# Masked lanes of a one-hot aggregation get an out-of-range row index, and each indirect gather gets a bound past which rows are skipped

## The chip, the cores and the metric

The kernel runs on one core of one Trainium2 chip. The metric is the device time of one execution in microseconds (us). Before the change it is 5670.04 us, the median of two runs (5664.36 and 5675.72 us).

## The reference

The reference is a stack of four graph layers over 6,250 nodes of 128 features and 106,250 edges, sorted by destination. Each layer takes `h = relu(layernorm(x))`, gathers a row of node data for the source of every edge, and sums something over the edges of each destination:

```python
# layer 0: attention; k, v are per node, q per node
a = (k[src] @ rel_att) . q[dst] * rel_pri / sqrt(16)         # per edge and head
h_agg = segment_sum(v[src] @ rel_msg * softmax_over_dst(a), dst)
# layer 1: degree-normalised sum
h = segment_sum(xs[src], dst)
# layer 2: gated messages
gates = sigmoid(x[src] @ W_src + x[dst] @ W_dst + edge_attr @ W_edge)
out = segment_sum(x[src] @ W_msg * gates, dst) / segment_sum(gates, dst)
# layer 3: mean of neighbours
summed = segment_sum(x[src], dst)
```

What matters here: four times over all edges, a row of a table in HBM is fetched by `src`.

## The kernel before

**Tiles.** Nodes are cut into 49 blocks of 128, plus one spare (`NS` = 50). The edges of a block are cut into tiles of 128 lanes; a tile starts at an edge number that is a multiple of 16, so its first lanes can belong to the block before, and its last lanes to the block after. There is room for `T` = 896 tiles. With this problem's edge list 856 tiles hold edges; the other 40 lie beyond the last edge. Of the 896 x 128 = 114,688 lanes, 106,250 hold an edge of their block and 8,438 (7.4%) do not. 133 tiles have at least one such lane: 40 have nothing else (5,120 lanes), and 93 have 3,318 between them.

**Order.** A pass over the edges takes the tiles in 224 quads of four. They are dealt out so that 16 neighbouring tiles in time lie 8 tiles apart in the edge list, within seven parts of 128 tiles each. The 40 tiles beyond the last edge therefore all fall into the last part, that is in the last seventh of each pass, five of them in every 16.

**The mask.** The prologue fetches, for each tile, 128 source numbers and 128 destination numbers, makes `RELF` (destination minus the block's first node) and `VAL` (1 where `RELF` lies in 0..127, else 0), lines 1118 to 1122. PE transposes `RELF` and `SRCF` so that a tile is a column; DVE copies them to `REL` (fp32) and `SRC` (int32), line 1137. In a pass, DVE makes the one-hot matrix `S` of a quad by comparing `REL` with a row of numbers (line 971). A lane that is not of the block matches nothing, so its row of `S` is zero, and whatever row was gathered for it adds nothing.

**The gathers.** For each quad, SP copies four columns of `SRC` to `ISLOT` (a ring of four slots); POOL waits for it, and for the consumer of the ring slot's last content, and issues four indirect DMAs of 128 rows each, one per tile (line 500):

```python
for j in range(QUAD):
    nc.gpsimd.indirect_dma_start(
        out=rows[:, slot, j, :], out_offset=None, in_=table,
        in_offset=bass.IndirectOffsetOnAxis(ap=ISLOT[:, slot, j:j + 1], axis=0),
    ).then_inc(s["gathered"][slot], 16)
```

There are four passes of 896 gathers: pass 0 (layer 0, table `tab2`, rows of 1,024 bytes), pass 2 (layer 1, `tab1`, 512 bytes), pass 3 (layer 2, `tab2`, 1,024 bytes), and pass 4 (layer 3, `tab1`, 512 bytes). Number 1 belongs to the messages of layer 0, which gather nothing by index. In passes 2 and 4 the ring slot comes free when PE has multiplied it (`agg_done`, line 688); in pass 0 when DVE has multiplied keys by queries (line 1257); in pass 3 when DVE has multiplied messages by gates (line 1331). The results of line 688 are added to an accumulator in SBUF by DVE, one tile at a time (line 988).

**Between the passes.** Layer norms, and projections by PE that write the tables (`dve_proj`, `pe_proj`, `sp_proj`, the latter at line 446). Pass 0 has six seams between its seven parts, at which the running maxima of the softmax are computed (`maxima`, `rescale`). The gathers of pass 0 start when both halves of `tab2` are stored (`proj[0]["stored"]`). `G`, the buffer that receives the gathers, also holds the index windows and the projection's staging in the prologue. POOL clears the accumulators with a memset (lines 537 and 561); DVE waits for that on the semaphore `acc_cleared`.

Of the kernel before, what the change touches and what calls it, by code (L numbers as in the profile page):

```python
# [8 lines left out]
ALU = mybir.AluOpType  # L9
# [3 lines left out]
P = 128  # L13
# [10 lines left out]
GROUP = 16  # L24
NEG = -1e30
PAD_NODE = 1 << 20


class Sizes:
# [25 lines left out]
def wait(eng, sem, value):  # L55

    if isinstance(value, int) and value <= 0:
        return
    eng.wait_ge(sem, value)  # L59


def build(nc, sz, a):
    NB, NS, T = sz.blocks, sz.slots, sz.tiles
    NQ, PARTS = sz.quads, sz.parts
    ctx = ExitStack()
    with ctx:
        def sb(name, shape, dt=F32):
            return ctx.enter_context(nc.sbuf_tensor(name, shape, dt))

        def sem(name):  # L70
            return ctx.enter_context(nc.semaphore(name))
# [20 lines left out]
        G = sb("G", [P, RING * QUAD * 2 * D])  # L92
# [58 lines left out]
        def at(i, u, d):  # L151

            v = u + d
            i = i + v // UNROLL if v // UNROLL else i
            v %= UNROLL
            return i * UNROLL + v, v % RING, i * (UNROLL // RING) + v // RING, v
# [4 lines left out]
        def steps(eng, fn, trailing):  # L161

            for u in range(UNROLL):
                fn(0, u)
            if sz.iters > 2:
                with eng.Fori(1, sz.iters - 1) as i:
                    for u in range(UNROLL):
                        fn(i, u)
            for u in range(UNROLL):
                fn(sz.iters - 1, u)  # L170
            for u in range(trailing):
                fn(sz.iters, u)
# [64 lines left out]
        def bc(ap, shape, dim):  # L237
            return ap.unsqueeze(dim).to_broadcast(shape)
# [15 lines left out]
        acc_cleared = sem("acc_cleared")  # L254
# [42 lines left out]
        SRCF = SCR[:, 0:T].rearrange("p (c e) -> p c e", c=NC)  # L297
# [3 lines left out]
        VAL = SCR[:, 2 * T:3 * T].rearrange("p (c e) -> p c e", c=NC)  # L301
# [179 lines left out]
        def registers(eng, row, q, most):  # L481

            _, values = nc.values_load_multi_w_load_instructions(  # L483
                row[0:1, bass.ds(q * QUAD, QUAD)], engines=[eng.engine], min_val=0, max_val=most,
                skip_runtime_bounds_check_because=reg_note)
            return values


        def pool_gathers(pool, n, rows, table):
            s = ps[n]  # L490

            def step(i, u):
                q, slot, turn, _ = at(i, u, 0)
                pool.wait_ge(s["idx_filled"][slot], (turn + 1) * 16)
                wait(pool, rows_read[n], q - RING + 1)
                if n == 0:
                    wait(pool, mv_stored[slot], turn * 16)
                pool.sem_inc(may_gather, 1)
                for j in range(QUAD):
                    nc.gpsimd.indirect_dma_start(  # L500
                        out=rows[:, slot, j, :], out_offset=None, in_=table,
                        in_offset=bass.IndirectOffsetOnAxis(ap=ISLOT[:, slot, j:j + 1], axis=0),
                    ).then_inc(s["gathered"][slot], 16)
            steps(pool, step, 0)

        @block.gpsimd
        def _(pool):
            nc.gpsimd.memset(ident[:, :], 0.0).then_inc(consts, 1)
            pool.wait_ge(consts, 1)
            nc.gpsimd.affine_select(out=ident[:, :], in_=ident[:, :], compare_op=ALU.not_equal, fill=1.0,  # L510
                                    base=0, pattern=[[-1, P]], channel_multiplier=1)
            nc.gpsimd.iota(iotaI, pattern=[[1, P]], base=0, channel_multiplier=0)
            nc.gpsimd.iota(thrI, pattern=[[P, NE]], base=0, channel_multiplier=0)
            nc.gpsimd.iota(pI, pattern=[[0, 1]], base=0, channel_multiplier=1)
            nc.gpsimd.iota(cI, pattern=[[8, NC]], base=0, channel_multiplier=0).then_inc(c_ready, 1)

            pool.wait_ge(windows_known, 1)
            pool.sem_inc(may_gather, 1)
            for c in range(NC):
                for src, dst in ((a["src_win"], SRCW), (a["dst_win"], DSTW)):  # L520
                    nc.gpsimd.indirect_dma_start(
                        out=dst[:, c, :], out_offset=None, in_=src,
                        in_offset=bass.IndirectOffsetOnAxis(ap=wI[:, c:c + 1], axis=0)).then_inc(windows_in, 16)

            pool.wait_ge(tiles_stored, 64)
            starts = flagd.rearrange("(m g t) e -> t m g e", m=PARTS, t=GROUP)
            with nc.allow_non_contiguous_dma(reason="single flags"):
                for h in range(HEADS):
                    for m in range(PARTS):
                        nc.gpsimd.dma_start(flags[h:P:HEADS, m, 0:sz.span].rearrange("t (g e) -> t g e", e=P),  # L530
                                            starts[:, m]).then_inc(flags_in, 16)

                    nc.gpsimd.dma_start(flags[h:P - HEADS:HEADS, :, sz.span:sz.span + 1], starts[1:GROUP, :, 0, 0:1]).then_inc(flags_in, 16)
                run = sz.chunk * GROUP
                if PARTS > 1:
                    nc.gpsimd.dma_start(LASTK[0:1, 1:PARTS], metad[2:3, run - 1:(PARTS - 1) * run:run]).then_inc(flags_in, 16)
            nc.gpsimd.memset(acc0, 0.0).then_inc(acc_cleared, 1)
            for r in range(2):
                pool.wait_ge(proj[0]["stored"][r], 16 * NS // 2)
            pool_gathers(pool, 0, G2, tab2)  # L540

            pool.wait_ge(scored["multiplied"], NQ)
            node, steps_done = [P, NS, D], [0]

            def each(out, x, y, op):
                nc.gpsimd.tensor_tensor(out, x, y, op).then_inc(pool_added, 1)
                steps_done[0] += 1
                pool.wait_ge(pool_added, steps_done[0])  # L550
            each(QT, H[:, :, :], ALPHA[:, :].unsqueeze(2).to_broadcast(node), ALU.mult)
            each(H[:, :, :], H[:, :, :], bc(ROWS[:, 3, :], node, 1), ALU.mult)
            each(X[:, :, :], X[:, :, :], H[:, :, :], ALU.add)
            each(X[:, :, :], X[:, :, :], bc(ROWS[:, 2, :], node, 1), ALU.add)

            pool.wait_ge(table_out, 16)
            pool_gathers(pool, 2, G1, tab1)

            pool.wait_ge(proj[2]["inputs"], 1)
            each(X[:, :, :], X[:, :, :], bc(ROWS[:, 0, :], node, 1), ALU.add)  # L560
            nc.gpsimd.memset(acc2, 0.0).then_inc(acc_cleared, 1)
            for r in range(2):
                pool.wait_ge(proj[2]["stored"][r], 16 * NS // 2)
            pool_gathers(pool, 3, G2, tab2)
            pool.wait_ge(table_out, 32)
            pool_gathers(pool, 4, G1, tab1)
# [392 lines left out]
        def _(dve):  # L959
            c = Chain(dve, dve_done)  # L960
            v_ = nc.vector
# [159 lines left out]
            c(v_.tensor_scalar(VAL, RELF, 0.0, None, ALU.is_ge))  # L1121
            c(v_.scalar_tensor_tensor(VAL, RELF, float(P), VAL, ALU.is_lt, ALU.mult))
            c(v_.scalar_tensor_tensor(KEYW, DKF, 1.0, VAL, ALU.add, ALU.mult))
            c(v_.tensor_scalar(KEYW, KEYW, -1.0, None, ALU.add))

            c(v_.tensor_copy(prev.unsqueeze(2), DSTW[:, :, 0:1]))
# [192 lines left out]
            layer_norm(X, H)  # L1319
            dve.wait_ge(w_next, 16 * 7)  # L1320
            dve_proj(dve, 2)
            dve.wait_ge(acc_cleared, 2)
            s = gated

            def step(i, u):
# [101 lines left out]
```

## Time and profile before

| what | value |
|---|---|
| median of the runs | 5670.04 us |
| span of the profiled execution | 6742.5 us |
| gathers | 3,584, in four stretches of 896 |
| stretches of gathers in the profile | 1577.6, 1316.6, 1551.4 and 1306.6 us |
| everything outside them | 990.3 us |

The time of the profiled execution is known only as its span, 6742.5 us, which is 1072 us (19%) over the median of the runs. The profile is therefore read for the durations of instructions and for what stands beside what, and the stalls in it with care.

### The profile page before, as it was taken

Reading aid. Unit: us, or ns where it says so; the run is one execution under the profiler, and the core shown is the slowest. Engines: PE = TensorE matmul, PEld = TensorE weight load, DVE = VectorE, ACT = ScalarE, POOL = GpSimd, SP = SyncE. Lnnn points to the kernel's source line nnn. Section 1 sums busy time; section 2 is a strip of 40 time slices with the busy share of each in tenths; the row PEclk is TensorE's granted clock in tenths of the full one; section 3 lists DMA queues with packets and bytes.
Section 4 is the critical chain, followed back from the end, with each engine's and each line's share of the span. In section 5 each row is a group of like instructions: output and inputs, shape, how many; then the busy total and the mean of one; then the engine's idle time right before and its main releaser. Section 6 shows DMA issues by size and latency. Waiting matters only on the chain. (4 is left out here: it accounts for less than half of the span.)

```text
span 6742.5 us, 78555 instructions
## 1 busy us (share of the span) xinstructions
PE 3183.9 (47%) x16832; PEld 2674.3 (40%) x16833; DVE 3229.3 (48%) x7806; ACT 663.9 (10%) x1525; POOL 3636.2 (54%) x3680
## 2 busy tenths in 40 slices
PE   4534445444453333333426777677775133333333
PEld 2324444443343333333324666566664122332322
DVE  6345665666785434343455444444446422322225
ACT  3111111111102000000001111111111000000002
POOL 3465555555601666666653555555553366666661
PEclk9767676766766555555558888888887555555556
DMA  2345445555521111111223444444443111111131
GB/s 66 103 128 152 142 138 152 144 140 141 126 59 31 44 46 44 46 45 45 45 29 107 112 114 115 113 113 114 113 111 75 49 45 44 46 45 45 46 45 27
DMA packets 598120, 563.89 MB, mean 84 GB/s; under 512 B 215476, under 2 KB 480350, under 8 KB 598016
## 3 DMA queue, kind: packets, MB, share of 16 engines
q0 software_dynamic: 145888, 355.31, 20.5%
q1 hardware_dynamic: 452128, 207.41, 12.3%
q8 instruction: 38, 0.62, 0.0%
q14 instruction: 66, 0.54, 0.0%
HBM read 478.69 MB, written 81.82 MB: 83 GB/s over the span
## 5 line engine op out<-in xcount | busy, mean ns | idle before, releaser
L500 POOL DMA_INDIRECT G<-tab,ISLOT x3584 | 3503.4, 978 | 2817.0 <-issue 1253.7
L988 DVE TENSOR_TENSOR ACCR<-ACCR,PSA 128x128 f32 (+2 forms) x3584 | 1142.7, 319 | 2244.9 <-remote 1597.7
L688 PE MATMUL PSA<-G,S 128*128 128x128 f32 x3584 | 905.9, 432 | 1133.8 <-DMA G<-tab,ISLOT 550.4
L688 PEld LDWEIGHTS PSA<-G,S 128*128 128x128 f32 x3584 | 779.6, 321 | 1210.4 <-DVE ACCR L988 554.1
L971 DVE TENSOR_TENSOR S<-iota,REL 128x512 f32<-128x512 f32 x1120 | 790.0, 706 | 10.5 <-issue 7.1
L688 PE MATMUL PSA<-FLG,S 128*128 128x256 f32 x1792 | 552.2, 463 | 6.9 <-DVE FLG L1331 2.7
L1331 DVE TENSOR_TENSOR FLG<-G,FLG 128x512 f32<-128x512 f32 x224 | 155.1, 692 | 789.9 <-ACT FLG L927 542.9
L815 PE MATMUL PB<-QTR,ST 128*128 x1792 | 321.9, 336 | 400.6 <-ACT ST L834 388.8
L679 PE MATMUL PB<-identb,S 128*128 128x128 bf16 x1792 | 206.1, 247 | 618.9 <-DVE S L971 402.0
L815 PEld LDWEIGHTS PB<-QTR,ST 128*128 128x128 f32 x1792 | 280.2, 238 | 417.1 <-issue 416.5
L688 PEld LDWEIGHTS PSA<-FLG,S 128*128 128x128 f32 x1792 | 408.8, 240 | 88.2 <-issue 16.6
L834 ACT CAST ST<-PB 128x512 f32<-128x512 bf16 x448 | 262.1, 585 | 1784.4 <-remote 895.2
L679 PEld LDWEIGHTS PB<-identb,S 128*128 128x128 bf16 x1792 | 139.4, 111 | 714.5 <-DVE S L971 460.8
L702 PE MATMUL PB<-SCR 128*128 128x50 bf16 x896 | 77.6, 218 | 730.1 <-DVE SCR L951 606.0
L688 PE MATMUL PSA<-SCR,S 128*128 128x137 f32 x1792 | 348.9, 352 | 92.0 <-DVE ACCR L988 71.2
L761 PE MATMUL PB<-QTR,ST 128*128 x1792 | 353.2, 358 | 39.2 <-issue 33.9
L702 PEld LDWEIGHTS PB<-SCR 128*128 128x128 bf16 x896 | 51.2, 116 | 788.6 <-DVE SCR L951 643.8
L688 PEld LDWEIGHTS PSA<-SCR,S 128*128 128x128 f32 x1792 | 317.6, 255 | 100.6 <-DVE SCR L1264 66.5
L761 PEld LDWEIGHTS PB<-QTR,ST 128*128 128x128 f32 x1792 | 306.1, 258 | 76.3 <-issue 76.0
L811 PE MATMUL PB<-W,SCR 128*128 128x128 f32 x1792 | 255.0, 286 | 42.9 <-issue 36.1
L811 PEld LDWEIGHTS PB<-W,SCR 128*128 128x128 f32 x1792 | 220.8, 194 | 62.4 <-issue 57.3
L392 ACT COPY G<-PB 128x384 f32<-128x384 f32 (+2 forms) x200 | 79.7, 398 | 1623.2 <-PE PB L374 1623.2
(241 smaller groups left out, 2688.8 us busy)
## 6 DMA issues: line engine op xcount, KB each, us to landing
G<-tab,ISLOT POOLq DMA_INDIRECT x3584
mvd<-G SPq DMA_DIRECT2D x224, 256.0 KB
MV<-mvd SPq DMA_DIRECT2D x224, 256.0 KB
SCR<-in_ea_t SPq DMA_DIRECT2D x896, 64.0 KB
ISLOT<-SRC SPq DMA_DIRECT2D x896, 2.0 KB
tab<-G SPq DMA_DIRECT2D x100, 128.0 KB, 1.7
tab<-H SPq DMA_DIRECT2D x2, 3200.0 KB, 13.8
out_x<-X SPq DMA_DIRECT2D x1, 3072.0 KB
```

The source lines that it names most:

```text
L392: nc.scalar.copy(HT[:, r, 0:ni, :].rearrange("p t d -> p (t d)"), PB[r][:, 0:ni * P]).then_inc(s["copied"], 1)
L500: nc.gpsimd.indirect_dma_start(out=rows[:, slot, j, :], out_offset=None, in_=table, in_offset=bass.IndirectOffsetOnAxis(ap=ISLOT[:, slot, ...
L679: last = nc.tensor.transpose(STP[par][:, j, :], bf_view(slot, j), identb[:, :])
L688: last = nc.tensor.matmul(PSA[:, par, j, 0:width], S[:, slot, j, :], rhs(j), start=True, stop=True)
L702: nc.tensor.matmul(HISTP, LOH[:, slot, j, :], HIH[:, slot, j, :], start=first, stop=final, skip_group_check=True)
L761: last = nc.tensor.matmul(QD[v % 2][:, j, :], ST[:, v % 2, j, :], QT[:, bass.ds(blocks[j], 1), :].rearrange("p o d -> p (o d)"), start=Tru ...
L811: nc.tensor.matmul(QD[v % 2][:, j, :], EA[:, slot, j, :], W[:, 4 * D:5 * D], start=j == 0, stop=False, skip_group_check=True)
L815: last = nc.tensor.matmul(QD[v % 2][:, j, :], ST[:, v % 2, j, :], QT[:, bass.ds(blocks[j], 1), :].rearrange("p o d -> p (o d)"), start=Fal ...
L834: nc.scalar.copy(ST[:, par, :, :], STP[bank]).then_inc(s["st_copied"], 1)
L971: return v_.tensor_tensor(S[:, slot, :, :], bc(iota[:, :], [P, QUAD, P], 1), REL[:, bass.ds(q * QUAD, QUAD)].unsqueeze(2).to_broadcast([P, ...
L988: v_.tensor_tensor(rows, rows, PSA[:, par, j, 0:width], ALU.add).then_inc(s["rows_added"], 1)
L1331: v_.tensor_tensor(RHS[:, v % 2, :, 0:D], G2[:, slot, :, D:2 * D], RHS[:, v % 2, :, D:2 * D], ALU.mult).then_inc(s["multiplied"], 1)
```

## The change

A lane with `VAL` = 0 gets the source number 2^20 in place of its own: two more DVE instructions in the prologue compute `(SRCF - 2^20) * VAL + 2^20`. Each gather of the four passes is given `bounds_check=NS * P - 1` (6,399, the last row of the table) and `oob_is_err=False`: a row whose index is greater is not copied. Since the lanes that are not copied keep what the buffer held, POOL clears `G` once, after the tables are stored and ahead of the first gather of pass 0, and waits for that memset. The semaphore count for which DVE waits ahead of pass 3 goes from 2 to 3. The gathers of the prologue's windows (line 521) have no bound.

```diff
+NO_ROW = 1 << 20
@@ pool_gathers: step
                     nc.gpsimd.indirect_dma_start(
                         out=rows[:, slot, j, :], out_offset=None, in_=table,
                         in_offset=bass.IndirectOffsetOnAxis(ap=ISLOT[:, slot, j:j + 1], axis=0),
+                        bounds_check=NS * P - 1, oob_is_err=False,
                     ).then_inc(s["gathered"][slot], 16)
@@ gpsimd
             for r in range(2):
                 pool.wait_ge(proj[0]["stored"][r], 16 * NS // 2)
+            nc.gpsimd.memset(G[:, :], 0.0).then_inc(acc_cleared, 1)
+            pool.wait_ge(acc_cleared, 2)
             pool_gathers(pool, 0, G2, tab2)
@@ vector, prologue
             c(v_.scalar_tensor_tensor(KEYW, DKF, 1.0, VAL, ALU.add, ALU.mult))
+            c(v_.scalar_tensor_tensor(SRCF, SRCF, -float(NO_ROW), VAL, ALU.add, ALU.mult))
+            c(v_.tensor_scalar(SRCF, SRCF, float(NO_ROW), None, ALU.add))
             c(v_.tensor_scalar(KEYW, KEYW, -1.0, None, ALU.add))
@@ vector, ahead of pass 3
-            dve.wait_ge(acc_cleared, 2)
+            dve.wait_ge(acc_cleared, 3)
```

## Rows read from the trace of the kernel before

**Rows 1.** The page: span, and POOL, clock and DMA in 40 slices.
```profile
span 6742.5 us, 78555 instructions
...
POOL 3465555555601666666653555555553366666661
PEclk9767676766766555555558888888887555555556
DMA  2345445555521111111223444444443111111131
```

**Rows 2.** Busy time by stretch: the four passes and what lies between them.
```profile
core 0: us, PE busy (x) PEld busy (x) DVE busy (x) ACT busy (x) POOL busy (x), PEclk, DMA share, GB/s
0.00:226.10 226.10, 123.81 (x484) 78.94 (x485) 130.42 (x374) 66.84 (x135) 54.94 (x90) 0.96 0.23 64
226.10:1803.70 1577.60, 725.57 (x4295) 627.62 (x4293) 896.44 (x1982) 204.50 (x563) 884.25 (x896) 0.69 0.52 142
1803.70:2160.20 356.50, 149.19 (x860) 129.57 (x859) 279.32 (x599) 65.51 (x182) 53.48 (x5) 0.66 0.16 45
2160.20:3476.80 1316.60, 507.04 (x2672) 435.69 (x2672) 526.45 (x1547) 0.00 (x0) 897.65 (x896) 0.52 0.20 45
3476.80:3617.60 140.80, 61.27 (x166) 24.20 (x166) 110.80 (x300) 25.97 (x83) 24.41 (x2) 0.72 0.16 48
3617.60:5169.00 1551.40, 1107.32 (x6208) 941.81 (x6208) 727.43 (x1538) 247.11 (x442) 857.73 (x896) 0.83 0.45 114
5169.00:5295.90 126.90, 13.45 (x60) 10.80 (x60) 102.19 (x115) 16.66 (x38) 0.07 (x1) 0.56 0.13 31
5295.90:6602.50 1306.60, 450.06 (x1784) 387.08 (x1784) 373.10 (x1110) 0.00 (x0) 863.60 (x896) 0.51 0.21 45
6602.50:6742.50 140.00, 46.15 (x308) 38.58 (x308) 83.11 (x243) 37.31 (x83) 0.08 (x1) 0.68 0.10 24
```

**Rows 3.** Timeline of POOL in pass 4: start, duration, idle before it.
```profile
5502.53 1.11 POOL L500 DMA_INDIRECT G<-tab,ISLOT  x1 [5.01 <-issue]
5503.95 0.95 POOL L500 DMA_INDIRECT G<-tab,ISLOT  x1 [0.30 <-issue]
5505.20 0.94 POOL L500 DMA_INDIRECT G<-tab,ISLOT  x1 [0.30 <-issue]
...
5532.01 1.07 POOL L500 DMA_INDIRECT G<-tab,ISLOT  x1 [4.64 <-remote]
```

**Rows 4.** Waits of POOL over the whole span: total, times, longest.
```profile
POOL G L500 <- issue: 1253.7, 3292, 6.5
...
POOL G L500 <- DVE FLG L1331: 329.9, 92, 7.2
POOL G L500 <- DVE SCR L1257: 328.0, 60, 22.5
```

**Rows 5.** All gathers, by source line: duration minimum, median and maximum.
```profile
L500 POOL DMA_INDIRECT G<-tab,ISLOT x3584: 938/945/2695, 226.1 to 6601.6; - x200
```

**Rows 6.** POOL's other DMAs and memsets, by line.
```profile
L530 POOL DMA_DIRECT2D FLG<-flagd x56 | 29.8, 600 | 38.9 <-DMA metad<-QTR 38.9
...
L561 POOL MEMSET ACCR<- 128x12800 f32 x1 | 10.8, 10766 | 0.1
...
L537 POOL MEMSET ACCR<- 128x6850 f32 x1 | 6.0, 5965 | 0.0
```

**Rows 7.** POOL's gathers of passes 2 and 4: first six sevenths, last seventh.
```profile
core 0: us, POOL busy (x), PEclk, DMA share, GB/s
2160.20:3288.00 1127.80, 769.14 (x768) 0.52 0.18 45
3288.00:3476.80 188.80, 128.51 (x128) 0.52 0.32 45
5295.90:6416.00 1120.10, 737.75 (x766) 0.51 0.18 45
6416.00:6602.50 186.50, 125.85 (x130) 0.53 0.34 46
```

**Rows 8.** Timeline of DVE where the mask is made.
```profile
81.24 0.63 DVE L1121 TENSOR_SCALAR SCR<-SCR 128x896 f32<-128x896 f32 x1
81.90 1.09 DVE L1122 SCALAR_TENSOR_TENSOR SCR<-SCR 128x896 f32<-128x896 f32 x1
83.02 1.09 DVE L1123 SCALAR_TENSOR_TENSOR G<-G,SCR 128x896 f32<-128x896 f32 x1
...
105.93 0.56 DVE L412 TENSOR_TENSOR G<-H,MASK 128x384 f32<-128x384 f32 x1 [12.81 <-DMA metad<-QTR]
```

**Rows 9.** Timeline of SP and of POOL at the start of pass 0.
```profile
214.60 8.81 SPq L446 DMA_DIRECT2D tab<-G  x5
223.45 2.48 SPq L596 DMA_DIRECT2D ISLOT<-SRC  x4
...
226.11 1.10 POOL L500 DMA_INDIRECT G<-tab,ISLOT  x1 [79.66 <-DMA ISLOT<-SRC]
```

**Rows 10.** DMA issues by line: KB each, median us to landing.
```profile
tab<-G SPq DMA_DIRECT2D x100, 128.0 KB, 1.7
```

## The prediction

> **What bounds the kernel now.** I read the page first, for its 40 slices. POOL is busy at five to six tenths through four long stretches, and nothing else is as busy through all of them; the DMA share changes between one and five tenths from stretch to stretch while POOL's does not [rows 1]. So the four passes are alike on POOL and unlike on everything else.
>
> The busy times by stretch say how alike. Each pass has 896 gathers; their busy time is 884, 898, 858 and 864 us, although passes 0 and 3 move rows of 1,024 bytes and passes 2 and 4 rows of 512. The passes last 1578, 1317, 1551 and 1307 us; the five stretches outside them add up to 226.1 + 356.5 + 140.8 + 126.9 + 140.0 = 990.3 us [rows 2]. PE is busy for 1107 of the 1551 us of pass 3, and DVE for 896 of the 1578 us of pass 0. They are the nearest next bounds [rows 2].
>
> The timeline of POOL shows what a gather costs when nothing holds it: 0.94 to 0.95 us of work and 0.30 us before the next one, so one starts every 1.25 us. The 0.30 us never goes away, and there is no more of it between quads, where POOL also waits on semaphores and adds to one: that housekeeping hides behind the gather that is running. About once in 30 gathers a gap of 4 to 5 us stands there, with no releaser, or with one called "remote" [rows 3].
>
> Is the unprofiled kernel bound by this? 3,584 x 1.25 = 4480 us. The median is 5670 us; less the 990 us outside the passes (if the profile stretches them little) that leaves 4680 us for the passes, 1.306 us per gather, and only 200 us above the floor. The profiled passes sum to 5752 us, so most of their gaps of 4 to 5 us cannot be in the unprofiled run. Of the 200 us, some 20 us at each of five or six seams of pass 0 (the longest wait for line 1257 is 22.5 us) make 100 to 120; the rest is for short waits on the ring in passes 0 and 3 [rows 4]. The page's chain of waits names a cause for only a few per cent of the span, and I do not build on it. So I take the kernel as paced by POOL's 1.25 us per gather, some 96% of the time of the passes. Whatever the change does to a gather's 0.945 us is multiplied by 3,584 and nearly all of it reaches the end: 1 ns per gather is 3.6 us, and 2% of the kernel is 32 ns per gather.
>
> **The change, part by part.** *Two DVE instructions in the prologue.* They have the shapes of lines 1122 and 1121: 1.09 and 0.63 us, with some 0.03 us between chained instructions, 1.8 us. The mask is made ahead of the stores for which line 412 then waits 12.8 us, so this is on the path [rows 8]: +1.8 us.
>
> *The memset of G.* It is 128 x 4,096 fp32. The two memsets of POOL cost 5.965 us for 6,850 columns (0.87 ns each) and 10.766 us for 12,800 (0.84 ns each), so this one costs about 3.5 us [rows 6]. It can start when the last store of the table has landed. SP issues five stores from 214.60 for 8.81 us, the last one at about 222.7, and they land in 1.7 us: 224.4 us. The first gather starts at 226.11 us today because it waits for its indices, issued at 223.45 [rows 9, 10]. The memset would end at about 227.9 and the semaphore adds a little: the first gather is late by about 2 us. Behind it queue only the gathers; DVE's wait for `acc_cleared` 3 ahead of pass 3 counts the same memset as before, and costs nothing. +2 us.
>
> *The bound itself, in the instruction.* If it needs a register to be set ahead of each gather, that is sequencer work, which is hidden today behind the running gather [rows 3]. 0 us; uncovered it would be some tens of ns each, and that is inside the upper end below.
>
> *The check, 3,584 times 128 indices.* No row shows a gather with a bound. The nearest rows are POOL's direct DMAs of line 530, which also write 128 pieces (16 partitions x 8 runs) and take 600 ns, and the gather without a bound, 945 ns [rows 5, 6]. Fetching, scaling and adding an index for 128 lanes thus costs some 345 ns. A check is part of the same walk. Lower bound of its price: 0, if the same walk compares anyway with a bound that is never reached. Upper bound: as much again as all the index work, 345 ns, 1236 us in all. Reading both ends, I take the value near 0, since the duration is so even (minimum 938, median 945 ns) that it looks like one fixed walk over 128 lanes.
>
> *The rows that are skipped.* 8,438 lanes per pass, 33,752 in four passes. Does POOL save their time? Upper bound: a gather's work is all per lane, 945 / 128 = 7.38 ns, so 33,752 x 7.38 = 249 us. Lower bound 0: the walk goes over 128 lanes whatever they bring. What the trace can tell is that the duration does not follow what is moved: in the last seventh, where nearly a third of the tiles hold no edge and fetch one and the same row 128 times, the DMA share rises from 0.18 to 0.32 and from 0.18 to 0.34, while POOL needs 1.004 and 0.968 us per gather against 1.001 and 0.963 before [rows 7]. I take 0, but it is the weaker of my choices. A loss is also possible, if a gather with skipped rows takes a slower way: it concerns 133 of 896 gathers, and at 345 ns more each it is 4 x 133 x 0.345 = 184 us.
>
> *The traffic that goes away*, 7.4% of 355 MB, frees DMA engines that are busy at 0.20 to 0.52 [rows 2]. In the last seventh the landings come sooner; PE waits less for them, but POOL sets the pace there too: 128 gathers in 189 us against 188 us on average in the six parts before [rows 7]. 0 us.
>
> For this last part a rule of the Trainium skill can be weighed. By "DMA: Bandwidth & Descriptors", section "Anatomy of one DMA", a DMA on POOL's path costs about 2.0 us plus bytes over 436 GB/s, and generating the descriptors is called small. By it skipping bytes would be the whole effect: 7.4% of 128 KB is 0.02 us per gather in passes 0 and 3 and half in the others, at most 58 us. The trace disagrees on what counts here, since generation takes 945 ns per gather with either row size, and it is what queues up [rows 2, 5].
>
> Sum: +1.8 +2 +0 +0 = about +4 us. Against the profiled execution that is 6742.5 to 6746 us; against the median of the runs, 5670 to **5674 us**.
>
> **Rivals.** *Case 1, the walk is the same (chance 0.39).* A lane costs POOL what it did, checked or not, copied or not; or a small price for the check and a small gain from the skip cancel. 5674 us, and 5560 to 5780 us around it. For it: the even duration. Against it: that two unknowns of many lanes both come out near nothing is a narrow target.
>
> *Case 2, skipped rows save their time and the check is free (0.31).* It holds if POOL tests every index already and leaves the lane at once. All of 7.38 ns saved: 5674 - 249 = 5425 us. Half of it (the index is still fetched): 5549 us. Passes 2 and 4 can take it, with PE and DVE busy for under half; pass 3 gives back part, as its PE work of 1107 us is just under its floor of 896 x 1.25 = 1120 us [rows 2]. For it: what is not written should not take time. Against it: rows 7. It falls under 2% if less than about half is saved.
>
> *Case 3, the check costs (0.30).* It is the one on the slower side. Place: the 0.945 us of every gather, 763 of 896 of which skip nothing and can win nothing back. At a quarter of the index work, 86 ns, it is 3,584 x 0.086 = 309 us: 5983 us. At half of it 6292 us, at all of it 6910 us. It decides from 32 ns per gather net. For it: descriptors here come from a program on POOL, and a compare and a branch per lane are instructions; two checks at 1 ns per lane are already beyond the point. Against it: a bound might be tested always.
>
> That the bound skips nothing, and row 2^20 is read, is not a rival for the time: it would be case 1.
>
> **How the numbers follow.** About 2% is what a measurement of this kernel can tell from no change. The predicted time is case 1's, 5674 us. Case 2 gives faster by over 2% in nearly all of its 0.31, say 0.29; case 3 gives slower by over 2% in 0.28 of its 0.30, with 0.01 more from the slow way of masked gathers in case 1; case 1 and the rims of the others give 0.42 within 2%. The range reaches to case 2's full gain, 5425, and to case 3 somewhat over a third of the index work, 130 ns, 6140 us. Beyond its ends lie about 0.04 below and 0.12 above. Case 1's own range is 5560 to 5780 us.
>
> **What would show it.** The median duration of line 500 in the profile after: 945 ns under cases 1 and 2, over 977 ns under case 3. The minimum and the durations in the last seventh of each pass: still 938 ns under case 1; under case 2 a second group well below 0.94 us, nearly a third of the gathers there, and that seventh shorter than the others. The 0.30 us between gathers should stay; if it grows, the register for the bound was not hidden. The DMA share in the last sevenths should fall from 0.32 to about 0.18. The prediction is wrong if a gather's work depends on the check or on the skip by more than 32 ns on average, or if POOL does not pace the unprofiled passes.

## The result and the profile after

The changed kernel takes 5913.19 us (median of 5905.78 and 5920.61), against 5670.04 before: a ratio of 1.043, with a 95% interval of 1.040 to 1.0459. It is slower by 243 us.

The engines in the rows are POOL (GpSimd, which issues the gathers), DVE (VectorE), PE (TensorE, PEld its weight loads), ACT (ScalarE) and SP (which issues the plain DMAs).

The first profiled execution of the kernel before spans 6742.5 us, that of the changed kernel 5904.0, about its median. So the gaps of 4 to 5 us on POOL in [rows 3] were of that one execution. A second profile of the kernel before, spanning 5669.4 us, has none of them, and the comparison is made with it. First the busy time by stretch of both (columns as in [rows 2]), the kernel before first.

```profile
core 0 of [0], span 5669.4 us
...
0.00:225.10 225.10, 123.64 (x484) 78.85 (x485) 130.43 (x374) 66.92 (x135) 55.09 (x90) 1.00 0.22 64
225.10:1468.40 1243.30, 709.61 (x4341) 603.59 (x4339) 906.81 (x1999) 216.31 (x569) 915.72 (x896) 0.76 0.67 181
...
1822.30:3009.10 1186.80, 498.53 (x2676) 455.53 (x2676) 531.29 (x1555) 0.00 (x0) 913.92 (x896) 0.50 0.23 50
...
3148.00:4284.10 1136.10, 941.19 (x6252) 789.62 (x6252) 751.46 (x1551) 250.32 (x447) 863.06 (x896) 0.99 0.60 155
...
4403.00:5529.30 1126.30, 461.54 (x1784) 396.99 (x1784) 372.32 (x1111) 0.00 (x0) 853.27 (x896) 0.50 0.24 53
```

And the changed kernel:

```profile
core 0 of [0], span 5904.0 us
...
0.00:232.30 232.30, 126.39 (x495) 80.92 (x497) 133.03 (x377) 68.08 (x137) 58.49 (x91) 1.00 0.22 62
232.30:1509.20 1276.90, 730.83 (x4333) 620.39 (x4331) 906.80 (x1999) 215.03 (x567) 954.68 (x896) 0.74 0.63 170
...
1857.80:3100.80 1243.00, 499.12 (x2676) 456.33 (x2676) 530.19 (x1558) 0.00 (x0) 970.33 (x896) 0.50 0.19 44
...
3235.70:4471.10 1235.40, 955.61 (x6255) 800.08 (x6256) 755.40 (x1553) 250.24 (x447) 962.21 (x896) 0.98 0.53 136
...
4586.30:5767.40 1181.10, 461.76 (x1784) 397.09 (x1784) 375.86 (x1114) 0.00 (x0) 908.38 (x896) 0.50 0.20 47
```

All of the loss is in the four passes: 4692.5 us before, 4936.4 after. Passes 0, 2, 3 and 4 lose 34, 56, 99 and 55 us, so the loss is not the same in each. Outside the passes the time falls, from 977 to 968 us: the first gather is 7 us later, and the four stretches behind the passes are 16 us shorter, 752 us before and 735 after. What shortens them comes out below, under "How much a skipped row saves". DVE, PE and ACT do the same work in nearly the same time. The DMA share falls, as there is less to move. What grew is POOL. Its gathers, by source line (duration minimum, median, maximum), before, in the second profile:

```profile
L500 POOL DMA_INDIRECT G<-tab,ISLOT x3584: 942/948/2636, 225.1 to 5528.2; - x200
```

and after, where an instruction of POOL's queue has joined them:

```profile
L501 POOLq MOVE  x3584: 29/29/38, 231.5 to 5751.1; - x200
L501 POOL DMA_INDIRECT G<-tab,ISLOT x3584: 992/998/2871, 232.3 to 5766.5; - x200
```

The median gather costs 50 ns more, and so does the shortest. The MOVE of 29 ns is taken here for the setting of the register for the bound, the sequencer work of which the forecast spoke. It is not what costs: in e5 below, where the bound is row 0, there is no MOVE, and the median gather is 998 ns as well. It is hidden, because the gap between gathers is still 0.30 us (timeline of POOL in pass 4, changed kernel):

```profile
4704.25 0.99 POOL L501 DMA_INDIRECT G<-tab,ISLOT  x1 [0.30 <-issue]
4705.55 0.99 POOL L501 DMA_INDIRECT G<-tab,ISLOT  x1 [0.30 <-issue]
```

50 ns x 3,584 is 179 us. The measured loss is 243. The mean duration grew more than the median: 989 ns in the second profile of before, 1059 ns after, 70 ns x 3,584 = 250 us. The groups by line, before and after:

```profile
L500 POOL DMA_INDIRECT G<-tab,ISLOT x3584 | 3546.3, 989 | 1705.5 <-issue 928.8 <-DMA ISLOT<-SRC 591.7 <-PE PSA L688 86.6
```

```profile
L501 POOL DMA_INDIRECT G<-tab,ISLOT x3584 | 3795.7, 1059 | 1616.6 <-issue 1037.0
```

So there are two questions. Which part of the change costs the 50 ns? And why do some gathers grow by far more than that?

### The profile page after: what moved, and what is told of

Same layout as the page of the kernel before. It is cut to its first block, busy times and chain, and to the rows that moved or that the text cites. A ratio compares the mean times of both kernels' runs of the same rounds, so it can differ in the third digit from the quotient of the medians.

```text
span 5904.0 us, 82142 instructions
## 1 busy us (share of the span) xinstructions
PE 3024.3 (51%) x16832; PEld 2540.5 (43%) x16833; DVE 3256.3 (55%) x7808; ACT 674.3 (11%) x1525; POOL 3931.6 (67%) x3681
## 3 DMA queue, kind: packets, MB, share of 16 engines
q0 software_dynamic: 145888, 329.53, 21.1%
## 4 chain that ended last, share of the span: by engine, by line
DMA 27%; issue 23%; PE 22%; DVE 12%; POOL 11%; ACT 2%; DVEq 1%; SPq 1%; POOLq 1%; ACTq 0%
DMA G<-tab,ISLOT 23%; PE PSA L692 14%; POOL G L501 11%; DMA ISLOT<-SRC 4%; PE PB L382 3%; DVE ACCR L992 2%; DVE S L975 1%; PE PB L815 1%; DVE ACCR L999 1%; PE PB L375 1%; PE PB L683 1%; PE PB L819 1%; ACT H L857 1%; DVE G L402 1%; DVE ACCR L1357 1%
## 5 line engine op out<-in xcount | busy, mean ns | idle before, releaser
L501 POOL DMA_INDIRECT G<-tab,ISLOT x3584 | 3795.7, 1059 | 1616.6 <-issue 1037.0
L692 PE MATMUL PSA<-G,S 128*128 128x128 f32 x3584 | 927.8, 440 | 1583.6 <-DMA G<-tab,ISLOT 1583.6
L692 PE MATMUL PSA<-FLG,S 128*128 128x256 f32 x1792 | 438.4, 389 | 4.8 <-DVE FLG L1337 3.9
L683 PEld LDWEIGHTS PB<-identb,S 128*128 128x128 bf16 x1792 | 114.6, 104 | 728.2 <-DVE S L975 680.5
L765 PE MATMUL PB<-QTR,ST 128*128 x1792 | 361.1, 364 | 48.2 <-issue 42.7
L692 PEld LDWEIGHTS PSA<-FLG,S 128*128 128x128 f32 x1792 | 331.2, 195 | 45.6 <-DVE FLG L1337 5.7
L765 PEld LDWEIGHTS PB<-QTR,ST 128*128 128x128 f32 x1792 | 308.3, 259 | 92.1 <-issue 92.1
L1263 DVE TENSOR_TENSOR SCR<-G,PB 128x512 f32<-128x512 f32 x224 | 153.7, 686 | 316.0 <-PE PB L765 131.6
L1345 DVE TENSOR_TENSOR SCR<-PB,G 128x512 f32<-128x512 f32 x224 | 154.9, 692 | 268.0 <-issue 128.8
L819 PE MATMUL PB<-QTR,ST 128*128 x1792 | 249.9, 285 | 0.0
L382 PE MATMUL PB<-W,G 128*128 128x128 f32 (+2 forms) x900 | 237.0, 393 | 0.6 <-DVE G L402 0.4
```

The lines of the kernel that those rows point to most:

```text
L382: last = nc.tensor.matmul(PB[2 + (1 - r)][:, 0:cols], HT[:, 1 - r, t, :], w(t), start=t == 0, stop=t == ni - 1)
L501: nc.gpsimd.indirect_dma_start(out=rows[:, slot, j, :], out_offset=None, in_=table, in_offset=bass.IndirectOffsetOnAxis(ap=ISLOT[:, slot, ...
L683: last = nc.tensor.transpose(STP[par][:, j, :], bf_view(slot, j), identb[:, :])
L692: last = nc.tensor.matmul(PSA[:, par, j, 0:width], S[:, slot, j, :], rhs(j), start=True, stop=True)
L765: last = nc.tensor.matmul(QD[v % 2][:, j, :], ST[:, v % 2, j, :], QT[:, bass.ds(blocks[j], 1), :].rearrange("p o d -> p (o d)"), start=Tru ...
L819: last = nc.tensor.matmul(QD[v % 2][:, j, :], ST[:, v % 2, j, :], QT[:, bass.ds(blocks[j], 1), :].rearrange("p o d -> p (o d)"), start=Fal ...
```

## Experiments

Theory A: a gather with a bound costs POOL a price of its own, whatever its indices are, and skipping a row gives POOL nothing. Rival B: the check is free and the skipped rows cost. Rival C: the new indices, the memset or the traffic matter. Theory D, formed on the traces of e0 and e1: the excess over the median is gathers held, that is kept waiting, by a DVE instruction that runs when they start. Rival E: that excess comes from the DMA side.

| label | what it is | us | ratio to before (95%) | gather, median and mean ns |
|---|---|---|---|---|
| e0_before_again | before | 5665.4 | 1.0001 (0.9991 to 1.0012) | 948, 989 |
| after | the change | 5913.2 | 1.043 (1.040 to 1.0459) | 998, 1059 |
| e1_check_only | bound alone | 5933.4 | 1.0465 (1.0445 to 1.0486) | 1000, 1069 |
| e2_index_only | indices and memset, no bound | 5675.8 | 1.002 (1.0011 to 1.003) | 948, 990 |
| e3_check_no_skip | the change, nothing skipped | 5931.9 | 1.0472 (1.0455 to 1.049) | 998, 1062 |
| e4_skip_half | bound at row 3199 | 5955.1 | 1.0501 (1.0479 to 1.0524) | 998, 1075 |
| e5_skip_all | bound at row 0 | 5780.2 | 1.0193 (1.0171 to 1.0215) | 998, 1029 |
| e6_check_is_err | bound alone, as an error | 6010.7 | 1.0599 (1.0576 to 1.0622) | 1015, 1087 |
| e7_check_small_onehot | bound alone, short compares | 5780.7 | 1.019 (1.0172 to 1.0209) | 1000, 1023 |
| e8_lanes64_plain | e2 with 64 lanes, no bound | 5516.9 | one run | 898, 949 |
| e9_lanes64_check | e3 with 64 lanes, bound | 5692.8 | one run | 937, 998 |
| e10_left_out | before, 36 gathers left out | 5621.2 | 0.9915 (0.9901 to 0.9928) | 949, 990 |
| e11_left_out_split | e10, compares split in four | 5549.5 | 0.9796 (0.9782 to 0.9809) | 945, 969 |

### The kernel before, again

> The kernel before, unchanged, for a second profiled execution. The first one spans 6742.5 us against a median of 5670 us, with gaps of 4 to 5 us on POOL about once in 30 gathers. If those gaps belong to that one profiled execution, as the forecast assumed, this one spans 5670 to 5720 us, its gathers keep a median of 945 ns and 0.30 us between them, and its four passes come out at 1120 to 1250 us each. If the gaps are part of the kernel, they are here again and the span is near 6700 us.

It spans 5669.4 us. The passes take 1243, 1187, 1136 and 1126 us, the rest 977 us. The forecast had reckoned 4680 us for the passes and 990 outside them. The median gather is 948 ns, 3 ns above that of the first profile.

### The bound alone, the indices alone, both with nothing skipped

e1 is the kernel before and one line:

```diff
                         in_offset=bass.IndirectOffsetOnAxis(ap=ISLOT[:, slot, j:j + 1], axis=0),
+                        bounds_check=NS * P - 1, oob_is_err=False,
```

> The kernel before with nothing but the bound on each gather; indices as before, so no row is skipped, and no memset. Theory A (the check is a flat price of each instruction, 998 against 945 ns whatever the indices): +53 ns x 3584 = +190 us at the least, and within 10 us of the changed kernel, so 5900 us, ratio 1.040. Rival B (skipped rows are what costs): gathers of 945 ns and ratio 1.00.

e2 is the changed kernel without that line and with an index that exists:

```diff
-NO_ROW = 1 << 20
+NO_ROW = 6399
-                        bounds_check=NS * P - 1, oob_is_err=False,
```

> The changed kernel without the bound; masked lanes get row 6399, the last of the table, instead of a number beyond it, so they are all fetched; the two DVE instructions and the memset stay. Theory A: gathers of 945 ns, only the prologue's 6 us (first gather at 232.3 instead of 226.1 us): 5676 us, ratio 1.001. Rival C (the new indices or the late start cost more than that, for instance by many lanes on one row): over 5700 us, ratio over 1.005.

e3 has the index 6399 and keeps the bound:

> The changed kernel with row 6399 for the masked lanes instead of a number beyond the table, so the bound is there and nothing is skipped. Against the changed kernel it tells what skipping itself does. Theory A (skipping gives POOL nothing): gathers of 998 ns, 5913 us within 10 us, ratio 1.043. If skipping saved or cost POOL time, this kernel would be slower or faster than 5913 us by up to 249 us.

e1 has all of the loss and 20 us more, e2 nearly none of it, and e3 is 19 us slower than the change itself, 5931.9 against 5913.2. Both e1 and e3 were expected within 10 us of it, and missed. The 50 ns are there in e1 and e3, where no row is skipped, and absent in e2. So the bound costs them, and rivals B and C fall. e2 prices the rest of the change at about 11 us (6 to 17).

The three steps add up: from 5665.4 us the indices and the memset lead to 5675.8, the bound to 5931.9 (256 us), and the skipping back to 5913.2 (19 us less; the intervals of the two ratios just touch). So skipping does give something, though the gather's median is 998 ns with it and without. In the profiles of e3 and of the changed kernel, 7 us of it are in the passes and 16 in the stretches behind them; the next section shows why.

### How much a skipped row saves

> The changed kernel with the bound at row 3199 instead of 6399, so about half of the real rows are skipped as well (those edges add stale rows; the layers' sums are not the reference's). Theory A (POOL walks all lanes alike, 53 ns for the check and nothing back): median gather 998 ns and 5913 us within 15 us. If a skipped lane saved its 7.4 ns and only the few of the changed kernel were too few to see: over 60 lanes less per gather, 0.5 us shorter, and the passes would fall until DVE or PE sets the pace, to under 5300 us.

> The same with the bound at row 0, so practically no row is copied at all (the sums are of stale rows). Theory A: gathers still 998 ns; the traffic of the gathers, 355 MB, goes away, and the time stays within 20 us of 5913 us, because transfers are not what paces the passes. If transfers or landings mattered, it would be clearly faster; if POOL saved the lanes, gathers would take half or less.

Both have the changed kernel's median of 998 ns: POOL gets nothing for a skipped row. The rows of the software queue (packets, MB, share of the engines) say what is left of it. Before, in the second profile:

```profile
q0 software_dynamic: 145888, 355.31, 24.8%
```

the changed kernel:

```profile
q0 software_dynamic: 145888, 329.53, 21.1%
```

and e5, which skips practically every row:

```profile
q0 software_dynamic: 145888, 4.87, 1.9%
```

The bytes go, the packets stay, to the last one. A packet is not a row, though: in the trace's packet records nearly every packet of rows moves 4,096 bytes before the change, 4 rows of 1,024 bytes or 8 of 512. In e5 nearly all of them move 16 bytes in passes 0 and 3 and 32 in passes 2 and 4, which is 4 bytes for each row. In the changed kernel 33,752 rows that shrink to 4 bytes account for 25.79 MB, and the queue moves 25.78 MB less. So a skipped row keeps its place in the packet, with 4 bytes in it. That POOL writes this place as it would any other is an inference from the equal medians.

What skipping does give shows behind the last gather of a pass, where PE waits for the rows to land. In the changed kernel, at the end of pass 4, the last gather ends at 5767.44 us and PE multiplies 1.2 us later:

```profile
5766.45 0.99 POOL L501 DMA_INDIRECT G<-tab,ISLOT  x1 [0.30 <-issue]
5768.66 2.08 PE L692 MATMUL PSA<-G,S 128*128 128x128 f32 x8 [3.17 <-DMA G<-tab,ISLOT]
```

In e3, where the masked lanes all fetch row 6399, it is 4.1 us (5785.13 to 5789.24):

```profile
5784.13 1.00 POOL L501 DMA_INDIRECT G<-tab,ISLOT  x1 [0.30 <-issue]
5789.24 2.08 PE L692 MATMUL PSA<-G,S 128*128 128x128 f32 x8 [4.60 <-DMA G<-tab,ISLOT]
```

The four stretches behind the passes sum to 749 to 752 us in the profiles of e0, e1, e2 and e3 and to 735 to 739 in those of the changed kernel, e4 and e5. That is the 16 us.

The expectations missed the totals: e4 is 42 us above the changed kernel, where at most 15 were expected, and e5 is 133 us below it, where at most 20 were. With equal medians, most of the difference is in the means (1075 and 1029 ns), that is, in the long gathers.

### The error flag

```diff
+                        bounds_check=NS * P - 1,
```

> The kernel before with the bound on each gather, but with an index past it declared an error instead of skipped silently (no index is past it). Theory A (any bound has the price): gathers of 998 ns, 5932 us as with the silent bound, ratio 1.047. Rival (the silent skip is a slower way of its own): gathers of 945 ns or near it and ratio 1.00 to 1.02.

The silent skip is not what costs; the flag for errors is dearer by another 15 ns per gather (1015 ns) and 77 us in all. The expectation missed that.

### What holds the long gathers

The trace of e1 in pass 4 shows one of them (start, duration, engine):

```profile
4715.72 1.00 POOL L500 DMA_INDIRECT G<-tab,ISLOT  x1 [0.30 <-issue]
4716.77 0.29 DVE L989 TENSOR_TENSOR ACCR<-ACCR,PSA 128x128 f32 x1 [3.17 <-PE PSA L689]
4716.97 0.68 DVE L972 TENSOR_TENSOR S<-iota,REL 128x512 f32<-128x512 f32 x1
4717.02 1.51 POOL L500 DMA_INDIRECT G<-tab,ISLOT  x1 [0.30 <-issue]
```

The one-hot compare of DVE (line 972 here) starts 0.05 us before the gather, and the gather takes 1.51 us. In the second profile of before, the same pair stands the other way round: the compare starts 0.24 us after the gather, and nothing happens.

```profile
4503.14 0.96 POOL L500 DMA_INDIRECT G<-tab,ISLOT  x1 [0.30 <-PE PSA L688]
4503.17 0.29 DVE L988 TENSOR_TENSOR ACCR<-ACCR,PSA 128x128 f32 x1 [3.14 <-PE PSA L688]
4503.38 0.68 DVE L971 TENSOR_TENSOR S<-iota,REL 128x512 f32<-128x512 f32 x1
```

Sorted over all gathers of pass 4 of e1 that have a compare near their start ("held" is the gather's duration over the median of 1000 ns):

```
compare starts relative to the gather   gathers   held, us   compare still runs for, us
-0.55 to -0.35                                5      0.108     0.236
-0.35 to -0.25                                6      0.242     0.371
-0.25 to -0.15                               12      0.362     0.488
-0.15 to -0.05                               32      0.484     0.612
-0.05 to -0.037                              11      0.515     0.642
-0.037 to 0.00                               44      0.010     0.721
 0.00 to  0.05                               66     -0.002     0.724
 0.05 to  0.30                               42     -0.002     0.771
```

The hold is what is left of the compare, less 0.13 us. The switch is sharp: a compare that has started 0.037 us or more before the gather holds it, a later one does not (one gather of the 44 is an exception, held for 0.519 us); in passes 2 and 3 the switch lies within 0.01 us of the same place. In the row from -0.037 to 0.00 it is the compare that takes longer, 0.74 us on average in place of 0.685. So it is something at the gather's very start that must wait.

The same sorting over all passes leaves little room for another cause. In the second profile of before, 526 of 3,584 gathers are more than 30 ns over the median, and 524 of them start while a DVE instruction with two inputs in SBUF runs: the compares (lines 971 and 947), the multiplies of lines 1264 and 1331, and at the seams of pass 0 the scans of the running maxima (lines 1181, 1195 and 1198), which hold a gather for 1.1 to 1.5 us on average. Of the 1,172 gathers that start under a DVE instruction with one input in SBUF and one in PSUM (lines 988, 1257 and 1339) not one is more than 14 ns over. In e1, 693 of 695 gathers over that mark start under an instruction with two inputs in SBUF. Summed over all gathers, the excess over the median is 147 us before and 219 us in the changed kernel. A bound only changes when POOL and DVE meet: in pass 3, 46 gathers of before start under the compare or the multiply of line 1331, and 207 of the changed kernel's do under the same two. e7 tests the theory:

```diff
-                return v_.tensor_tensor(S[:, slot, :, :], bc(iota[:, :], [P, QUAD, P], 1),
+                e = P if n < 2 else 8
+                return v_.tensor_tensor(S[:, slot, :, 0:e], bc(iota[:, 0:e], [P, QUAD, e], 1),
...
```

> The kernel before with the bound on each gather, and in passes 2, 3 and 4 the one-hot compare of line 971 over 8 columns instead of 128 (the rest of the matrix stays as pass 0 left it; the sums are not the reference's). It shortens that DVE instruction from 0.70 us to about 0.1. Theory D (a gather that starts while this DVE instruction runs is held until it ends, which made 399 gathers of the bounded kernel over 1.3 us long, against 153 without a bound, and is the 20 ns per gather by which the whole cost exceeds 53 ns): in passes 3 and 4 nearly no gather over 1.1 us, mean down from 1.093 and 1.030 to 1.00 to 1.01 us, in pass 2 down in part (two more DVE compares of bf16 remain); passes shorter by 80, 25 and some 30 us, in all 5933 down to about 5800 us. Rival E (the long gathers come from the DMA rings or from elsewhere): they stay as many and the time within 20 us of 5933 us.

The mean gathers of passes 2, 3 and 4 fall from 1089, 1093 and 1030 ns to 1013, 1014 and 1000 ns, the passes by 68, 71 and 27 us, and the whole by 153 us. Passes 3 and 4 do as expected; pass 2 gains more than twice the 30 us expected. Pass 0, left as it was, keeps 1275 us (1276). The row by line:

```profile
L500 POOL DMA_INDIRECT G<-tab,ISLOT x3584 | 3665.4, 1023 | 1698.6 <-issue 1092.1 <-DMA ISLOT<-SRC 500.0 <-DVE SCR L1259 49.2
```

Theory D stands, and rival E falls. The Trainium skill has a rule that fits, in "GPSIMD Engine Reference", section "Key points": GpSimd shares its SBUF interfaces with VectorE, and contends with DVE instructions that have two SBUF inputs. The trace agrees on which instructions hold a gather (524 of 526 above, and none with an input in PSUM); that the shared interface is the reason, no run here shows.

Holds also account for most of e4 and e5. Summed over the passes, gathers are held for 219 us in the changed kernel, 276 in e4 and 110 in e5, so +57 and -109 us; POOL's waits at the seams of pass 0 are 14 and 19 us shorter. Together that is the +44 and -128 us by which their passes differ in the profiles. Their DVE work is the same, and what differs is when the rows land, and so when PE and DVE follow. It is not that earlier landings are always good: gathers more than 0.3 us over the median number 74, 163, 153 and 31 in passes 0, 2, 3 and 4 of the changed kernel, 99, 169, 61 and 143 in e4, and 88, 0, 4 and 1 in e5, whose pass 4 is still 14 us longer than the changed kernel's, because 190 of its gathers are held for 0.1 to 0.3 us. Which meeting of POOL and DVE a kernel falls into was not predicted by anything here.

### What a lane costs

```diff
-                        out=rows[:, slot, j, :], out_offset=None, in_=table,
-                        in_offset=bass.IndirectOffsetOnAxis(ap=ISLOT[:, slot, j:j + 1], axis=0),
+                        out=rows[0:64, slot, j, :], out_offset=None, in_=table,
+                        in_offset=bass.IndirectOffsetOnAxis(ap=ISLOT[0:64, slot, j:j + 1], axis=0),
```

> The kernel before with gathers of 64 lanes instead of 128 (the upper half of each tile keeps what the cleared buffer held; the sums are not the reference's), no bound. It prices a lane. If the 945 ns are all per lane: 473 ns. If they are a fixed part of some 600 ns and the rest per lane (a direct DMA of 6 elements took 676 ns): about 770 ns.

> The same with the bound. If the check is a price of each lane (0.41 ns): 27 ns more than without the bound. If it is a price of the instruction: 53 ns more, as with 128 lanes.

The lines shown are e8's against the changed kernel, without the line of the bound, which e8 drops and e9 keeps. Without the bound, and with it:

```profile
L501 POOL DMA_INDIRECT G<-tab,ISLOT x3584: 891/898/2947, 230.4 to 5376.4; - x200
```

```profile
L501 POOL DMA_INDIRECT G<-tab,ISLOT x3584: 930/937/2784, 230.0 to 5552.2; - x200
```

Their pairs with 128 lanes are e2 (948 ns) and e3 (998 ns). Both expectations for the unbounded gather missed: half the lanes save 50 ns of 948. By a straight line through the two points a lane costs 0.78 ns, and some 848 ns do not depend on the lanes; a third count of lanes was not run. The check costs 39 ns for 64 lanes and 50 to 52 for 128, by a straight line some 27 ns for the instruction and 0.2 ns per lane, between the two expectations. What POOL does in them the trace doesn't show.

### A gather left out whole

The worst list of edges fills 884 tiles, and the kernel has room for 896. With no bound, e10 leaves out the gathers of the 12 tiles that no data can fill, in passes 2, 3 and 4, unrolls the last part of these passes and counts the fewer arrivals in the waits:

```diff
+        def never_used(t):
+            part, r = t // (sz.chunk * GROUP), t % (sz.chunk * GROUP)
+            return part * sz.chunk * GROUP + (r % GROUP) * sz.chunk + r // GROUP >= sz.most
...
                 for j in range(QUAD):
+                    if n and isinstance(q, int) and never_used(q * QUAD + j):
+                        continue
                     nc.gpsimd.indirect_dma_start(
...
-                pe.wait_ge(s["gathered"][slot], (turn + 1) * 64)
+                pe.wait_ge(s["gathered"][slot], arrived(n, slot, turn + 1))
...
```

> The kernel before, with no bound, that leaves whole gathers out where no data can need them: the room of 896 tiles is rounded up from the 884 that the worst list of edges can fill, so 12 of 896 tiles, all in the last part, are never used; passes 2, 3 and 4 issue no gather for them, and the waits of the last part count the fewer arrivals. Theory A (the gather as an instruction is the unit of price, its rows are not): 36 gathers x 1.25 us = 45 us less, 5663 down to 5618 us, ratio 0.992. If the pace of the last parts were set by PE or DVE, nothing: ratio 1.000.

5621.2 us, 0.9915: 36 gathers less are worth 49 us by the medians (45 expected), while 33,752 skipped rows, the contents of 264 gathers, save POOL nothing and give back the 19 us between e3 and the change. For POOL the gather is the unit of price.

### Shorter compares, with everything computed

e11 is e10 with the one-hot compare of passes 2, 3 and 4 in four instructions; the other compare of pass 2 (line 947) is split in the same way:

```diff
...
+                for j in range(QUAD):
+                    part = v_.tensor_tensor(S[:, slot, j, :], iota[:, :],
+                                            REL[:, bass.ds(q * QUAD + j, 1)].to_broadcast([P, P]), ALU.is_equal)
+                return part.then_inc(ps[n]["onehot_ready"], 1)
```

> The kernel with the never-used gathers left out and no bound, in which the one-hot compares of passes 2, 3 and 4 (line 971, and line 947 of pass 2) are four DVE instructions of 128 columns instead of one of 512; everything is computed as before. Theory D (a gather that starts under such a compare is held for the rest of it): the holds get about a quarter as long, the mean gather of pass 2 falls from 1.023 us to about 0.97 and those of passes 3 and 4 to 0.95; 45 to 60 us less than 5621, about 5570 us, ratio to the kernel before 0.983. If the gaps between four instructions leave the hold as it was, or DVE's extra time comes onto the path: 5621 us or more.

5549.5 us, 0.9796 (0.9782 to 0.9809), faster than both kernels of this study. The mean gathers of passes 2, 3 and 4 are 951, 954 and 945 ns, against 1023, 960 and 955 in e10; pass 2 gains 64 us of the 72. That is more than the 45 to 60 us expected. DVE takes 0.89 us instead of 0.68 for the four compares and has the time:

```profile
4482.21 0.29 DVE L1009 TENSOR_TENSOR ACCR<-ACCR,PSA 128x128 f32 x1 [2.91 <-PE PSA L703]
4482.25 0.94 POOL L515 DMA_INDIRECT G<-tab,ISLOT  x1 [0.30 <-PE PSA L703]
4482.41 0.89 DVE L992 TENSOR_TENSOR S<-iota,REL 128x128 f32<-128x128 f32 x4
4483.22 1.14 DVE L1009 TENSOR_TENSOR ACCR<-ACCR,PSA 128x128 f32 x3
4483.49 0.94 POOL L515 DMA_INDIRECT G<-tab,ISLOT  x1 [0.30 <-issue]
```

The gather at 4483.49 starts under the additions of line 1009 and is not held.

## Why the prediction was right or wrong

The measured 5913 us lies in the stated range of 5425 to 6140 us. That says little, as the range holds a gain of 4% as well as a loss of 8%. The forecast itself, 5674 us and no change, was wrong, and by the prediction's own last paragraph it is wrong: the check costs more than 32 ns per gather. What came is the rival on the slower side, case 3, which had 0.30. The step that failed is the check, put near 0; it costs 50 ns per gather, and 256 us in all with the holds that it brings (e3 against e2).

- *What bounds the kernel*: right. POOL paces the passes; 4680 us were reckoned for them and 4693 are in the second profile, and the gaps of [rows 3] were no part of the kernel. Dividing the 1.306 us per gather into 1.25 and short ring waits was wrong in one thing: of the 200 us above the floor, about 147 are held gathers (mean 989 against median 948 ns, x 3,584), and only some 55 are waits at the seams of pass 0, where 100 to 120 were reckoned. The holds already showed in the first profile of before, as a mean of 978 ns over the median of 945 [rows 5]. The prediction did not ask what they were.

```profile
L500 POOL DMA_INDIRECT G<-tab,ISLOT x3584 | 3503.4, 978 | 2817.0 <-issue 1253.7 <-DMA ISLOT<-SRC 608.8 <-DVE FLG L1331 329.9
```

- *The prologue*: +4 us was forecast. The first gather starts at 232.3 us against 225.1, and e2 prices the whole at about 11 us. The memset takes 3.51 us as reckoned, but starts at 227.85 and not at 224.4, when the last store has landed, and 0.96 us pass behind it:

```profile
227.85 3.51 POOL L542 MEMSET G<- 128x4096 f32 x1 [78.84 <-DMA tab<-G]
232.32 1.09 POOL L501 DMA_INDIRECT G<-tab,ISLOT  x1 [0.96 <-POOL G L542]
```

- *The register for the bound*: right. A MOVE of 29 ns per gather is there and is hidden.
- *The check*: here the forecast failed. The price was taken "near 0, since the duration is so even". An even duration says that a gather's work doesn't depend on its data. It says nothing on what one more step in that work costs. The bounds, 0 to 345 ns, held the 50 ns measured, and the point from which it decides (32 ns) was passed. Case 3's own value, 86 ns and 309 us, was high for the check and lacked the second term.
- *The missing term*: a gather that takes 50 ns longer meets DVE at other moments. Held gathers add 70 - 50 = 20 ns per gather, 71 us. In pass 3 they grow from 13 to 68 us, on top of 45 us for the bound, so it loses 99 us; in pass 0 they shrink from 66 to 60 us and its waits at the seams by 5, so it loses only 34.
- *The skipped rows*: 0 was right for POOL, and for the reason taken from [rows 7]. But the upper bound was wrong by ten: 7.38 ns per lane assumed that all of the 945 ns are per lane, and a lane costs 0.78 ns by the straight line. By that, all skipped lanes together could save POOL no more than 33,752 x 0.78 = 26 us, 0.5%. Case 2 had no room for its 0.31. The 600 ns of line 530 were read as work for 128 pieces [rows 6], and the direct DMA of six elements at line 536 was in the same answer of the trace with 676 ns; two rows with different counts of pieces and the same time would have shown that the time is not per piece.
- *The traffic*: it is gone as forecast; in the last sevenths of passes 2 and 4 the DMA share is 0.15 in both, against 0.39 in pass 4 of the second profile of before, and POOL's pace there did not care. What the 0 us left out is the end of each pass, where POOL no longer sets the pace: there PE can start on the last rows about 3 us sooner, and the four stretches behind the passes are 16 us shorter together.

## What to carry to other kernels

Where POOL paces a kernel with indirect DMAs, count instructions, not rows: here a bound costs some 50 ns on every gather of 128 rows and skipping rows saves POOL none, while a gather left out gives back its whole 1.25 us. Before pricing a share of an instruction, find two rows of it with different sizes; a duration that is even shows a fixed amount of work, not a free place for more. And where a mean stands clearly over the median of the instruction that sets the pace, look for what runs on the neighbouring engine when it starts.

## What the runs showed of the hardware

- An indirect DMA of 64 lanes took 898 ns on POOL, one of 128 lanes 948 ns: 0.78 ns per lane between the two.
- A bound costs 39 ns with 64 lanes and 50 to 52 ns with 128; declared as an error it costs 67 ns, with no index past it.
- A skipped row keeps its place in its packet, with 4 bytes: 145,888 packets with 355.31 MB, with 329.53 MB, and with 4.87 MB.
- With rows skipped, PE starts on the last rows of a pass 1.2 us after POOL's last gather; with the masked lanes all fetching row 6399 it is 4.1 us.
- A gather that starts while DVE runs a 128x512 compare of two SBUF operands is held for the rest of that instruction less 0.13 us, up to 0.5 us; scans with two SBUF operands held gathers for over 1 us. One that starts before the compare, or less than about 0.04 us after its start, is not.
- Not one of 1,172 gathers that started under a DVE instruction with one operand in PSUM was held (second profile of before, at most 14 ns over the median).
